# The distance between scores, turn and values' products in three pipelined attentions: three steps against two

## What is computed

```
scores = q @ k.T * scale            (level 0: + shifted position scores)
attn   = softmax(scores)            (102 x 102)
out    = attn @ v                   (head width 16 in levels 0 and 1, 64 in level 2)
H      = concat(out over heads) @ w_o
```

## Time and profile before

| | us |
|---|---|
| median of 3 runs | 1841.75 (1832.12 to 1842.03) |
| the profiled execution's own time | 1837.04 |
| its span, first to last instruction | 1835.2 |
| PE busy in the span | 1501.2 (82%) |
| DVE busy | 682.6 (37%) |
| ACT busy | 671.9 (37%) |
| POOL busy | 379.4 (21%) |

### The profile page before, as it was taken

The page is one execution under the profiler, slowest core; times in us unless marked ns, Lnnn a source line. Parts: engine busy times, 40 slices in busy tenths (PEclk is TensorE's granted clock), DMA queues, the critical chain, the costliest instruction groups (busy, mean ns, idle before and its releaser), DMA issues.

```text
span 1835.2 us, 31049 instructions
## 1 busy us (share of the span) xinstructions
PE 1501.2 (82%) x10048; PEld 1073.6 (58%) x10048; DVE 682.6 (37%) x1998; ACT 671.9 (37%) x2211; POOL 379.4 (21%) x449
## 2 busy tenths in 40 slices
PE   6878777478686777888985899499999998699993
PEld 4655545343222455666675788266676776588883
DVE  4454555621111465444336122244344224511112
ACT  1757656110000234777531112155456432113231
POOL 5212112100000122222101354121122000123331
PEclk8789889568777688999995799699999999569997
DMA  7422422629998400000006354200000200225543
GB/s 201 131 72 65 130 65 65 211 83 355 336 312 255 136 1 0 1 0 0 0 12 160 104 171 131 59 2 0 0 0 0 103 1 18 84 80 151 159 129 93
DMA packets 92812, 177.81 MB, mean 97 GB/s; under 512 B 35306, under 2 KB 53904, under 8 KB 90680
## 3 DMA queue, kind: packets, MB, share of 16 engines
q1 hardware_dynamic: 78528, 129.86, 24.3%
q10 hardware_dynamic: 7056, 30.67, 5.0%
q0 software_dynamic: 7136, 16.10, 3.0%
HBM read 149.61 MB, written 26.99 MB: 96 GB/s over the span
## 4 chain that ended last, share of the span: by engine, by line
PE 48%; issue 26%; DMA 9%; DVE 8%; POOL 4%; ACT 3%; SPq 2%; POOLq 0%; DVEq 0%; ACTq 0%
PE bank L1671 12%; DMA WM<-in_fc 6%; PE bank L2125 6%; PE bank L2113 5%; PE bank L2115 4%; PE bank L1761 3%; PE bank L1790 2%; PE bank L1773 2%; PE bank L1800 2%; PE bank L2081 2%; SPq L215 1%; DMA WM<-rows_out 1%; POOL RS L630 1%; POOL ON L644 1%; PE bank L2100 1%
## 5 line engine op out<-in xcount | busy, mean ns | idle before, releaser
L1671 PE MATMUL bank<-XT,AREA 96*128 96x408 f32 (+1 forms) x640 | 239.0, 532 | 33.5 <-ACT XT L1434 16.2
L1671 PEld LDWEIGHTS bank<-XT,AREA 96*128 96x128 f32 (+1 forms) x640 | 121.9, 196 | 139.7 <-issue 99.7
L1761 PE MATMUL bank<-KZ,QT 128*102 128x102 f32 x1152 | 141.3, 262 | 10.3 <-ACT PB L1478 5.7
L630 POOL TENSOR_TENSOR RS<-VE,expo 102x4 f32<-102x4 f32 (+1 forms) x53 | 53.0, 1001 | 464.7 <-DVE VE L835 403.6
L1761 PEld LDWEIGHTS bank<-KZ,QT 128*102 128x102 f32 x1152 | 122.6, 175 | 22.9 <-issue 12.1
L644 POOL TENSOR_TENSOR PB<-PB,RCU 102x306 f32<-102x306 f32 x96 | 66.9, 696 | 289.4 <-DVE RCU L896 289.4
L2125 PE MATMUL bank<-WM,KZ 128*128 x660 | 120.2, 330 | 0.0
L2113 PE MATMUL bank<-KZ,SLOTS 128*128 128x128 f32 x660 | 115.9, 300 | 2.5 <-issue 2.5
L2125 PEld LDWEIGHTS bank<-WM,KZ 128*128 128x128 f32 x660 | 107.9, 193 | 0.4
L2113 PEld LDWEIGHTS bank<-KZ,SLOTS 128*128 128x128 f32 x660 | 93.5, 198 | 16.6 <-issue 5.4
L751 POOL DMA_INDIRECT rows_out<-KZ,TARGET x66 | 66.7, 1010 | 172.5 <-DVE KZ L1307 136.6
(11 more groups left out here) (314 smaller groups left out, 2779.5 us busy)
## 6 DMA issues: line engine op xcount, KB each, us to landing
AREA<-in_fc SPq DMA_DIRECT2D x10, 1536.0 KB, 24.2
SLOTS<-in_m3w SPq DMA_DIRECT2D x33, 384.0 KB
WM<-in_fc ACTq DMA_DIRECT2D x5, 2304.0 KB, 18.4
WM<-in_fc SPq DMA_DIRECT2D x6, 1536.0 KB, 26.2
AREA<-in_fc ACTq DMA_DIRECT2D x4, 2304.0 KB, 20.4
SLOTS<-in_m1w SPq DMA_DIRECT2D x33, 256.0 KB
AREA<-pos_scratch SPq DMA_DIRECT2D x16, 459.0 KB
pos_scratch<-AREA SPq DMA_DIRECT2D x8, 913.5 KB
```

Source lines behind the costliest of these rows:

```text
L630: pool.tensor_tensor(RS[0:rows, 0:width], VE[0:rows, 0:width], expo[0:rows, half, 0:width], ALU.pow).then_inc(sem["power_out"], at.one("po ...
L1671: last = pe.matmul(dst, lhsT, rhs, start=n == 0, stop=n == len(pieces) - 1)
L1761: last = pe.matmul(psum[k][0:T, cols(j)], QT[:, tile, cols(bb)], KALL[:, unit % per_tile * (HEADS // per_tile) + tile, cols(bb)], start=Tr ...
```

## The change

In all three attentions the turn of a unit follows its scores by two steps in place of three, the copy by ACT by three in place of four, the values' products by four in place of five, and the copy of the result by DVE by five in place of six. The projections move one step down with them, and a pass has one step fewer (22 for 23 on PE). The index of PT is written so that unit and buffer still agree. No operation, size, bank or buffer is added or removed.

```
-        STEPS = UNITS + 7
+        STEPS = UNITS + 6
...
-            return min(UPB * bb + UPB + 6 + i, STEPS - 1)
+            return min(UPB * bb + UPB + 5 + i, STEPS - 1)
...
                 for s in range(STEPS + 1):
-                    n = s - 6
+                    n = s - 5
                     if 0 <= n < UNITS and av_filled(dv, n % UPB):
...
-                for s in range(UNITS + 4):
-                    if 0 <= s - 4 < UNITS:
+                for s in range(UNITS + 3):
+                    if 0 <= s - 3 < UNITS:
                         k = at.bank(TBANKS)
                         src = full(k)[0:T, 0:TU].rearrange("p (h t) -> p h t", h=HPU)
-                        free(activation(PT[s % 2][:, 0:HPU, :], src, ACT.Copy), k)
+                        free(activation(PT[(s - 3) % 2][:, 0:HPU, :], src, ACT.Copy), k)
...
-                    n = s - 5
+                    n = s - 4
                     if 0 <= n < UNITS:
                         bb, unit = n // UPB, n % UPB
                         f = fill_of(dv, n)
...
-                    n = s - 3
+                    n = s - 2
                     if 0 <= n < UNITS:
                         pe.wait_ge(sem["probs_ready"], at.take("probs_ready"))
                         k, p = claim(TBANKS)
```

## The result

The changed kernel takes 1858.59 us (median of 4 runs, 1852.43 to 1868.87) beside 1840.72 us for the kernel before (median of 4, 1832.12 to 1842.03): a ratio of 1.0111, 95% interval 1.0072 to 1.0150. The forecast was 1850.0 in a range of 1837 to 1862: the median lies in the range, but the change costs 1.1% where 0.45% (8.2 us) was forecast. The profiled execution took 1852.43 us with a span of 1850.6 us, 15.4 more than before (1835.2).

The account below looks back on a forecast made before the run. PE, busy 1501.2 of 1835.2 us, was taken as the bound, its work unchanged. Levels 1, 2 and 0 gave +6.6 + 3.6 - 2.0 = +8.2 us on the profiled 1837.04, 1845.2; forecast median 1850.0, range 1837 to 1862.

Parts of the forecast that it names:

- The way from scores to turn: Chain through DVE, ACT, DVE and POOL: 3.58 us, leaving no slack in level 1's steady two-step order at 1.30 a step.
- start: Beginning of a level 1 pass: PE idles 1.74 us before turn 0 and 0.42 before turn 2; +1.0 us a pass.
- Steady: Middle of a level 1 pass: turns 4 and 6 each about 0.15 late while the pipeline settles; +0.3 us.
- End: End of a level 1 pass: 3.07 us of PE work between scores 15 and turn 15 against 3.58; +0.5 us.
- 0.14 for the saved projection: Level 1 pass: one more step has scores followed by a projection, taking 0.54 instead of 0.68; -0.14 us.
- rival A: Clock falls after the longer starting idle in each level 1 and 2 pass, 1.7 us each; total 1863.6, chance 0.13.
- -0.4: Level 0's first six steps: turn and values' products come a step earlier and use up gaps; about -0.4 us.
- Rival B: Level 0's unit 8 stall vanishes whole, with the clock's fall behind it: 10.6 us less; total 1841 or 1836, chance 0.12.
- C: No difference: start waits are regained later in each pass because DVE or ACT had paced it; 1842, chance 0.09.
- D: One drain step of about 1 us saved in each of twelve passes: -12 us, 1830, chance 0.04.

Follow-up runs that it names:

- shortpool: l12only with POOL multiplying only 4 of 102 columns of each head in levels 1 and 2; 1838.83 us in one run.
- lead: l12only with turn 0 put back behind the fourth unit's scores in levels 1 and 2; 1842.98 us in one run.
- copy2: Changed kernel rewritten with a distance table, two steps in all levels, same instruction lists; 1857.63 us, 1.0085 to the kernel before.
- l12only2: l12only again, timed beside fill2; 1852.52 us, 1.0070 to the kernel before.
- l12only: Kernel before with two steps in levels 1 and 2 only, three in level 0; 1852.12 us, ratio 1.0070.
- fill: l12only with six useless products ahead of the first turn's wait in levels 1 and 2; 1836.29 us in one run.
- fill2: The same kernel as fill, timed in 12 runs; 1847.20 us, 1.0026 to the kernel before.
- l0only: Kernel before with two steps in level 0 only, three in levels 1 and 2; 1845.32 us, ratio 1.0037.
- l0only2: The same kernel as l0only, timed in more runs; 1842.13 us, 0.9996 to the kernel before.
- l0copy: Kernel before, three steps everywhere, with only DVE's copy of the result one step earlier in level 0; 1839.02 us, ratio 0.9990.
- l0fill: Kernel before, three steps everywhere, with six useless products in each level 0 pass's stall; 1841.83 us, ratio 0.9998.
- copy3: Control: kernel before rewritten with a distance table, three steps in all levels, same instruction lists; 1845.15 us, ratio 1.0017.

## Why the prediction was right, and where not

**The way from scores to turn: right.** The chain of 3.58 us put the first turn at an idle stretch of 1.74, and 1.74 and 1.96 are what levels 1 and 2 show. shortpool confirms the chain as the cause.

**Level 1: the sign and the waits right, the size a third too large.** Of the terms, *start* was +1.0 and measured (1.74 + 0.27) - (0.61 + 0.34 + 0.18) = +0.88. *Steady* was +0.3 for turns 4 and 6 late by about 0.15 each, and they are late by 0.18 and 0.14. *End* was +0.5 and measured (0.28 + 0.47) - 0.30 = +0.45, the 0.30 being the projection's wait there before the change. But the forecast put this wait ahead of turn 15, which waits for nothing; it stands ahead of turn 14 and of the projection, so the size of *end* is in part luck. With the 0.14 for the saved projection the terms make +1.5 a pass as measured (1.65 as forecast), and the pass grew by 1.2: 4.9 us, not 6.6.

What the sum had wrong is the sentence that 1.30 us a step is "exactly what PE's own work takes". In the changed kernel a step in which nothing waits takes 1.25 (739.14 to 740.39). In the kernel before, the values' products of the steady steps started 0.05 us after ACT's copy of the turned probabilities had ended (734.58 + 0.46 = 735.04):

```profile
734.58 0.46 ACT L1472 ACTIVATE PT<-bank 102x306 f32<-102x306 f32 x1
735.09 0.38 PE L1790 MATMUL bank<-PT,V 102*32 102x102 f32 x6
```

The next three copies end at 736.33, 737.63 and 738.93, and the products start at 736.38, 737.68 and 738.98. So it was ACT's copy, and not PE's own work, that released them each 1.30 us. PE's rows there show no idle time, because so short a wait is not printed. The change takes these four waits of 0.05 away, which gives back 0.2 of the missing 0.3; the rest stays open. What `lead` adds is that the terms can't be treated one by one: without the start's stall the second turn waits 0.51 where it waited not at all, and the pass gets only 0.3 of the 0.9 back. Where a chain is as long as the loop around it, a stall that is taken away at one place comes again at the next.

**Level 2: right at full clock, and rival A on top.** The forecast was +0.9 a pass; passes at full clock took 33.0 for 32.2, +0.8. The second turn's wait was 0.07 us for a forecast 0.24. In the sum I gave nothing for the clock. It fell to 0.95 in two passes of the changed kernel, in three of copy2 and l12only2 and in all four of l12only, each time for 1.3 to 1.5 us. This is rival A, priced at 1.7 us for each of eight passes; it holds for level 2, in part, and never for level 1, whose passes all show 1.00. The forecast of +10.2 for levels 1 and 2 meets +10.7 in the profile by errors that cancel: 1.7 too much in level 1 and 0.5 in level 2 at full clock, 2.7 left out for level 2's clock.

What the engine did before it fell: idle stretches of 1.96 us ahead of turn 0 (1.86 in the last pass) stand at the start of sixteen passes in four profiles, and the clock fell in twelve of them (two, three, three and four of four). With stretches of 0.83, 0.35 and 0.51 it fell in two of four (lead), with those of the kernel before (0.83 and 0.35, then about 0.18), of shortpool (1.48) and of fill and fill2 (0.80) in none. Level 1's sixteen passes with 1.74 in the same four profiles kept the full clock; why is open. The Trainium skill, "TensorE: Matmul & The Clock Gate", section "What's actually happening", says that the slow state is the default and activity releases the clock from it; level 2 and fill agree, and whether a given pass falls was not the same for the same order of instructions.

**Level 0: the waits right, the gain absent.** The copy's wait went, a wait for POOL of 1.03 came (forecast about 1.0), and `finish` waits 1.18 (forecast 0.9). I balanced this to -0.5 a pass. Two measurements of level 0 alone give -0.04% and +0.37%: -2 us is neither seen nor excluded by the one, and excluded by the other. The passes show what was mis-sized. PE's idle time in a pass up to its last projection, by what it stood ahead of, in us, mean of the second to fourth passes (24 with three steps, 12 with two, as above):

| ahead of | three steps | two steps |
|---|---|---|
| values' products | 3.13 | 1.29 |
| position products | 1.28 | 0.75 |
| scores | 0.42 | 0.00 |
| turn | 0.00 | 1.69 |
| projection | 0.32 | 1.54 |
| sum | 5.15 | 5.27 |

The gaps of the first steps shrank by 0.5, as the "-0.4" had it, and the values' products gained 1.8. What ate both are the turn and the projection, +1.7 and +1.2. The step that failed is the one that counted a single late turn of about 1.0, at unit 8, and a single late `finish` of about 0.9: a second turn waits 0.50 for POOL some 4 us ahead of it, and a second `finish` waits 0.40 (both in the changed kernel's second pass).

Rival B is out as a whole: its 10.6 us, 0.58%, lie below the intervals of both l0only and l0only2. Of its two prices taken alone, the copy's 1.38 and the clock's 1.7 a pass, neither l0copy nor l0fill shows a gain, and their intervals (down to -0.44% and -0.36%) don't exclude one of that size. What they do show is where the time goes: to the scores, which wait for the exponentials behind the load, and to PE's idle time.

**Rivals C and D** are out: the passes of levels 1 and 2 grew, and no pass there got shorter with the step that is gone. C's mechanism, that ACT had paced the steps, is real in a small part, the 0.2 us a pass told above.

**The sum.** +8.2 was forecast on 1841.75, and about twice that was measured: the range held the median because it was wide enough for a part of rival A. The two comparisons of the whole change give 1.0111 and 1.0085, 16 to 20 us, with levels 1 and 2 alone at 1.0070 twice, 13 us. The passes of levels 1 and 2 hold 10.7 us of it in the changed kernel's profile and 12.9 in that of l12only. The rest, 0.15 to 0.41% beyond l12only, for level 0 or for nothing at all, lies within what the intervals leave open: the same lists with another name (copy3) gave 1.0017 (0.9990 to 1.0043). I leave it open. No variant beats the kernel before: the best, l0copy at 0.9990 and l0only2 at 0.9996, can't be told from it.

## What to carry to other kernels

Before a software pipeline is made one step shorter, add up the chain through all its engines and compare it with the steps that remain; here 3.58 us stood against two steps of 1.30 and the turn's place, and a chain half a microsecond shorter would have made the same change almost free. Count at the pass's two ends first, since there the work that covers the chain is missing; but don't expect to win a stall back by filling one gap if the chain has no slack anywhere. A row without idle time doesn't show that the engine sets its own pace: compare its starts with the ends of what it waits for. And profile a kernel that is the same but for its name before crediting a stage with a gain: two executions can differ by more than the change does.

## What the runs showed of the hardware

- Six short products of no use (about 1.2 us) at the start of a pass kept TensorE at its 2.4 GHz level through a pass of 33 us, where the same pass after 1.96 us of idle time ran at a mean of 0.95 in twelve cases of sixteen, with one stretch at 0.50 behind the idle time. Level 1, after 1.74 us of idle time, never fell.
- In level 0's third pass the granted clock was 0.98 in place of 0.93 and the pass as long as before (40.8 us): PE's busy time fell by 0.84 us and its idle time rose by 0.74.
- For a step of level 1 (six score instructions, three turns, six of the values' products) PE takes 1.25 us at full clock where nothing waits, and 1.30 where the values' products start just behind ACT's copy.
- The same 16 sets of weights took 200.1 us in one execution and 210.0 in another of the same lists; from one execution to the next this stage varies by about as much as the whole change costs in its passes (10.7 us).
